# Top layer of a CIN tower: its second and third run of matmuls joined into one at the end

## The reference, cut to what matters

```
x1 = einsum('hjk,bjd,bkd->bhd', W0, e, e)  + b0
x2 = einsum('hjk,bjd,bkd->bhd', W1, e, x1) + b1
x3 = einsum('hjk,bjd,bkd->bhd', W2, e, x2) + b2
z  = concat(x1.sum(2), x2.sum(2), x3.sum(2))        # 512 x 384
h  = relu(concat(z, dense_ctx) @ W_top1 + b_top1)   # 512 x 512
h  = relu(h @ W_top2 + b_top2)                      # 512 x 256
y  = h @ W_top3
```

## Time and profile before

| what | value |
|---|---|
| median of 3 runs | 667.33 us (667.11 to 667.49) |
| profiled execution, own time | 667.98 us |
| its span | 666.2 us |
| TensorE busy (PE) | 644.0 us, 97% |
| VectorE (DVE) | 457.2 us, 69% |
| ScalarE (ACT) | 480.6 us, 72% |
| GpSimd (POOL) | 497.3 us, 75% |

### The profile page before, as it was taken

How to read it: one execution, slowest core, us unless ns; L and a number is a source line. 1 busy time by engine, 2 the same in 40 slices (tenths; PEclk the granted TensorE clock), 3 DMA queues, 4 the chain that set the end, 5 groups by cost and what they waited for, 6 DMA issues and landing times.

```text
span 666.2 us, 11234 instructions
## 1 busy us (share of the span) xinstructions
PE 644.0 (97%) x2676; PEld 478.7 (72%) x2676; DVE 457.2 (69%) x1183; ACT 480.6 (72%) x1737; POOL 497.3 (75%) x467
## 2 busy tenths in 40 slices
PE   3599999999999999999999999999999999999998
PEld 1387677777777777777787777777777777779873
DVE  1467777778686968777725786868687777774820
ACT  1457678878787969697834787878796978784912
POOL 5888888979797988888844797979888885553620
PEclk9989999999999999999999999999999999999999
DMA  6643515151514234142400514132241404002000
GB/s 160 143 107 71 125 25 118 36 121 13 140 15 98 58 68 86 38 115 36 119 11 2 119 13 113 20 78 55 47 85 17 115 10 118 4 4 90 5 1 1
DMA packets 68263, 43.32 MB, mean 65 GB/s; under 512 B 49482, under 2 KB 61709, under 8 KB 66457
## 3 DMA queue, kind: packets, MB, share of 16 engines
q1 hardware_dynamic: 56870, 38.04, 25.1%
q0 software_dynamic: 5184, 1.29, 2.3%
q10 hardware_dynamic: 6158, 3.45, 2.0%
HBM read 39.58 MB, written 1.96 MB: 62 GB/s over the span
## 4 chain that ended last, share of the span: by engine, by line
PE 94%; DMA 3%; SPq 1%; DVE 1%; ACT 1%; issue 1%; POOL 0%; ACTq 0%
PE a_ps L704 40%; PE d_ps L704 25%; PE quad_ps L655 14%; PE g_ps L745 5%; PE quad_ps L758 5%; PE a_ps L871 1%; PE quad_ps L672 1%; DMA rows<-x_first 1%; DMA emb<-tables_dram,rows 1%; PE quad_ps L659 1%; PE d_ps L842 1%; DMA x_first<-emb 1%; DMA picks_sb<-picks_dram 1%; PE rows_ps L842 0%; PE a_ps L842 0%
## 5 line engine op out<-in xcount | busy, mean ns | idle before, releaser
L930 ACT ACTIVATE parts<-a_ps,xt 128x128 f32<-128x128 f32 x1536 | 424.2, 383 | 104.5 <-PE a_ps L704 101.2
L551 DVE SCALAR_TENSOR_TENSOR parts<-d_ps,xt,parts 128x128 f32<-128x128 f32 x704 | 201.8, 343 | 108.2 <-PE d_ps L704 107.8
L311 POOL TENSOR_TENSOR parts<-parts 128x512 f32<-128x512 f32 x128 | 163.8, 1297 | 97.8 <-ACT parts L930 97.0
L704 PE MATMUL a_ps<-w_hi,x_hi 128*128 128x512 f32 x384 | 181.5, 473 | 0.6 <-issue 0.6
L311 POOL TENSOR_TENSOR left<-parts 128x512 f32<-128x512 f32 x128 | 166.8, 1319 | 6.5 <-ACT parts L930 4.9
L285 POOL DMA_INDIRECT emb<-tables_dram,rows_now x150 | 144.6, 964 | 25.2 <-issue 17.9
L704 PE MATMUL a_ps<-w_hi,x_lo 128*128 128x512 f32 x384 | 152.3, 397 | 0.6 <-DVE x_lo L520 0.6
L704 PE MATMUL a_ps<-w_lo,x_hi 128*128 128x512 f32 x384 | 151.5, 395 | 0.0
L704 PE MATMUL d_ps<-w_hi,x_hi 128*128 128x512 f32 (+1 forms) x256 | 127.1, 496 | 0.0
L655 PE MATMUL quad_ps<-products,w_sb 117*128 117x512 f32 (+1 forms) x210 | 107.3, 591 | 0.0
L704 PE MATMUL d_ps<-w_lo,x_hi 128*128 128x512 f32 (+1 forms) x256 | 97.7, 382 | 0.6 <-ACT xt L908 0.6
(11 more groups left out here) (72 smaller groups left out, 426.1 us busy)
## 6 DMA issues: line engine op xcount, KB each, us to landing
shifted<-x_rows SPq DMA_DIRECT2D x45, 312.0 KB
shifted<-x_rows SPq DMA_DIRECT2D x45, 234.0 KB
diag<-xt SPq DMA_DIRECT2D x240, 4.9 KB
rows<-x_rows SPq DMA_DIRECT2D x45, 78.0 KB
emb<-tables_dram,rows_now POOLq DMA_INDIRECT x150, 3.2
w_sb<-w_dram SPq DMA_DIRECT2D x6, 384.0 KB
shifted<-x_first SPq DMA_DIRECT2D x12, 136.5 KB
g_sb<-w_dram ACTq DMA_DIRECT2D x2, 768.0 KB, 9.4
```

The source lines that it names most:

```text
L311: nc.gpsimd.tensor_tensor(to, parts[:, i % 2, now:now + GF, :], parts[:, i % 2, more:more + GF, :], ALU.add).then_inc(pool_added, 1)
L551: nc.vector.scalar_tensor_tensor(now, d_ps[d % D_RING][:, H * at:H * (at + 1)], xt[:, u, i, j:j + 1], before, ALU.mult, ALU.add).then_inc( ...
L704: return nc.tensor.matmul(bank[:, 0:H * len(fields)], x[:, u, 128 * i:128 * (i + 1)], w[:, fields[0]:fields[-1] + 1, :].rearrange("p j h - ...
L930: last = nc.scalar.activation(parts[:, i % 2, 2 + GF * a + at, :], a_ps[(NA * i + a) % A_RING][:, H * at:H * (at + 1)], ACT.Copy, scale=xt ...
```

## The change

`PARTS` and `PART_AT` change. Before, the top layer ran three times: over chunks 0 to 7 (256 columns of G) in the body of chunk 8, over chunks 8 to 11 (128 columns) in the body of chunk 15, and over chunks 12 to 15 (128 columns) behind the last body. Now it runs twice: over chunks 0 to 7 where it did, and over chunks 8 to 15 (256 columns) behind the last body. The numbers of the parts and of the stores that are waited for are adapted.

```
-PARTS = [(0, HALF_CHUNKS), (HALF_CHUNKS, CHUNKS - 4), (CHUNKS - 4, CHUNKS)]
-PART_AT = {HALF_CHUNKS: 0, CHUNKS - 1: 1}
+PARTS = [(0, HALF_CHUNKS), (HALF_CHUNKS, CHUNKS)]
+PART_AT = {HALF_CHUNKS: 0}
...
-            layer2(2)
+            layer2(1)
...
-            pe.wait_ge(z3_stored, 3)
+            pe.wait_ge(z3_stored, 2)
...
-            store_z3(2)
+            store_z3(1)
```

## The result

The changed kernel takes 671.38 us (median of 6 runs, 669.88 to 672.83) against 667.41 us (6 runs, 666.45 to 668.21): the ratio is 1.0059, 95% interval 1.0042 to 1.0076. It is slower by 4.0 us. Forecast were 670.2 us and slower by 2.9.

The account below looks back on a forecast made before the run. TensorE was taken to bound the kernel. Last G -5.1 us plus joined run +7.95 us gave +2.85, said as +2.9: 670.2 us, slower by 0.43%; own range 669.4 to 671.4, with rival B 668.0 to 672.0.

Parts of the forecast that it names:

- The wait at the cast: Last body, block 2: ScalarE's context cast, moved earlier, waits 3.4 us for the context loads.
- SyncE's queue stays: Last body: copies to diag and the loads behind them keep their times, last context load issued at 614.30.
- The landing: Last context load, issued on SyncE at 614.30, takes 4.0 us and lands at 618.3.
- TensorE's pause: Start of block 3, last body: TensorE idles about 3 us until ScalarE frees a bank.
- The last G: End of the last body: G comes 5.1 us earlier instead of 8.6, as ScalarE's delay arrives in full.
- The joined run: Behind the last body: 256 columns take 16.65 us, +7.95 us there; joining saves 0.67 us in all.
- Rival D: A run costs by its matmuls, not its columns: 8.7 us for the joined one, 662.2 us, chance 1%.
- rival C: Clock falls in TensorE's new pause, nearly 7 us at half, G 2.9 us later: 673.1 us, chance 9%.
- its lead over ScalarE: Last body: TensorE's work ends about 0.6 us ahead of the last G, against 0.1 us before.
- the ring of banks: Allowance of some 0.5 us in the forecast's own range of 669.4 to 671.4 us.
- Rivals A and B: A: no wait at the cast, 666.7 us, 6%; B: shorter wait or ScalarE catching up, about 668.7 us, 9%.

Follow-up runs that it names:

- the pause filled: Changed kernel with six useless matmuls of 256 columns ahead of block 3's first group in the last body: 670.67 us, ratio 1.0042.
- the repeat: Changed kernel run once more, unaltered, against the kernel before: 670.82 us, ratio 1.0048.
- before_loads_later: Kernel before, short runs kept, with loads of W_top1 and all behind it held back until ScalarE staged block 1's fifth group: 671.59 us, ratio 1.0063.
- joined_pause_halved: Changed kernel with three useless matmuls ahead of block 3 in the last body, leaving TensorE a pause of 1.43 us: 670.34 us, ratio 1.0045.
- joined_loads_later: Changed kernel with loads of W_top1 and all behind it held back until ScalarE staged block 2's second group: 675.62 us, ratio 1.0122.
- joined_cast_later: Changed kernel with ScalarE's context casts moved behind block 3's first group, VectorE's low parts one group later: 669.39 us, ratio 1.0029.
- joined_ctx_before_wt: Changed kernel with the six context loads issued ahead of W_top1 and W_top2, still behind the last copies to diag: 667.44 us, ratio 0.9995.

## Why the prediction was right, and where it was short

- **Direction and cause: right.** The wait at the cast was forecast at 3.4 us and is 3.55, and it makes the whole loss, together with the fall of the clock that follows its pause: take it away and 667.24 us are left; put it into the old kernel and it takes 671.59.
- **SyncE's queue stays: right.** The landing was put at 618.3 in a program where G stood at 604.00; in the new trace the cast starts at 617.88, with G at 603.38, so 14.5 against 14.3 us behind G.
- **TensorE's pause: right in place, a little long.** About 3 us forecast, 2.73 and 2.92 seen.
- **The last G: -5.1 us forecast for the wait alone.** The cast itself is 4.99 us earlier behind the first G, and with the pause filled the way from it to the last G is unchanged (14.57 against 14.62): there the last G is 632.59 - 603.73 = 28.86 us behind the first in place of 34.11, so -5.25, of which 0.21 is the earlier landing. Right to 0.15.
- **The joined run: +7.95 us forecast, +8.12 measured.** From 634.75 to 651.59 it takes 16.84 us, against 16.65 in chunk 8. The saving is 0.5 to 0.6 us and not 0.67. Rival D is out.
- **The term that was mis-sized is the clock.** The forecast gave the fall of the clock 9% as rival C and nothing in the sum, since the only pause that was known to bring it had 5 us. It came in both profiles of the change. Rival C's price was wrong as well: 2.9 us, with nearly 7 us at half as in the earlier trace rows. The clock was at half for 3.4 us, so TensorE lost 1.7, of which its lead over ScalarE (0.6 us forecast) covered a part; 0.8 us reached the last G, and 0.6 in the repeat. The sum in the trace is -4.99 + 0.78 + 8.12 = 3.91, where -5.1 + 7.95 = 2.85 was forecast: 0.8 us of the difference is the clock, 0.1 the landing and 0.2 the joined run. The medians stand 3.97 and 3.22 us over their kernels before. The median of 671.38 lies at the upper edge of the forecast's own 669.4 to 671.4, an edge that was drawn for a later landing and the ring of banks. That it covered a fall of the clock was luck.
- **Rivals A and B** didn't come: the cast had its idle time, and ScalarE regained nothing in the last block; it stood idle 0.61 and 0.26 us more there for the slow TensorE.
- **Two readings of the trace were wrong, without weight in the sum.** The earlier trace rows have 37 slices with TensorE at nine tenths, not 39, and only the third with the clock lower. And 5.02 us was not TensorE's only wait: the same trace has 1.14, 0.91 and 0.57 us between 20 and 25 us, with the clock at its full level behind them. They would have been the nearest rows for a short pause.

The Trainium skill's sentence on pauses ("TensorE: Matmul & The Clock Gate", "Why this matters for your kernels") deserved more weight than the 9% that rival C had. The traces agree with its warning, and behind shorter pauses than the one that the page names: the fall came behind 2.73, 2.92 and 1.82 us. The two figures that the prediction took from the same page's "Back-to-back issue gap" don't fit this kernel's matmuls: 128 more columns cost 8.1 us in 39 of them.

## What to carry to other kernels

Work that is taken off the bounding engine moves everything behind it forward, except what hangs on a queue that something earlier releases; so before it is removed, the slack of each such landing is to be read (here 5.2 us, which no list of waits shows) and compared with the move (8.6 us). Work in the middle of a chain may be the cover of a wait that doesn't exist yet. And a new pause of the bounding engine is to be priced twice, with its own length and with the clock behind it; if it can't be avoided, filling it with useless matmuls keeps the clock, which was worth 0.8 us in the trace.

## What the runs showed of the hardware

- TensorE's clock fell to half behind pauses of 2.92, 2.73 and 2.50 us, and behind one of 1.82 us (before_loads_later). It stayed full behind one of 1.43 us (joined_pause_halved), behind one of 1.68 us near the start of joined_loads_later (at 21.5 us), and behind the two of 1.32 and 0.61 us in the one profile of joined_cast_later. The only fall in the trace of the kernel before had a pause of 5.02 us. Whether the length of the pause alone decides isn't shown.
- The fall doesn't come at a fixed distance: 1.5 us behind the restart in the changed kernel, about 1 us behind it in before_loads_later, and in the pause itself in the repeat and in joined_loads_later. The clock was at half for 3.4 us in the first three and for nearly 7 in the last.
- A load of 32 KB landed 1.8 us behind its issue with nothing large ahead of it in SyncE's queue, and 4.1 to 5.2 us behind it with 1.25 MB (768 KB and 512 KB) just ahead. The order in the queue gave more than the issue did: in joined_ctx_before_wt the last one was issued 1.5 us earlier and landed 3.8 us earlier, 10.7 us behind G of chunk 14 against 14.5 in the change.
